# A two-layer graph network with mixing and experts: gates as sums on VectorE, row copies chunk by chunk, a table load moved, and zero products at three stage ends

## What is computed

```python
w = jnp.einsum('rb,bio->rio', att, basis)            # 30 bases, 2 relations
for r in range(NUM_RELATIONS):
    gate = jax.nn.sigmoid(x_j @ gate_w[r, :, 0])     # one number of each row and relation
    msgs.append(gate[:, None] * x_j @ w[r])
msg = jnp.where((edge_type == 0)[:, None], msgs[0], msgs[1])
agg = jax.ops.segment_sum(msg, row, num_segments=x.shape[0])
return agg + x @ root + bias
```

## Time and profile before

| | |
|---|---|
| Median of 3 runs | 1045.41 us (1041.83 to 1046.39) |
| Profiled execution, its own time | 1051.21 us |
| Span of the profiled execution | 1049.4 us |
| Mean granted clock of TensorE | 0.963 of 2.4 GHz |
| Busy: TensorE, VectorE, ScalarE, GpSimd | 93%, 51%, 38%, 9% of the span |
| Moved by transfers | 120.46 MB |

### The profile page before, as it was taken

The page is one execution under the profiler, slowest core; times in us unless marked ns, Lnnn a source line. Parts: engine busy times, 40 slices in busy tenths (PEclk is TensorE's granted clock), DMA queues, the critical chain, the costliest instruction groups (busy, mean ns, idle before and its releaser), DMA issues. The chain is left out here.

```text
span 1049.4 us, 12457 instructions
## 1 busy us (share of the span) xinstructions
PE 980.8 (93%) x4787; PEld 632.9 (60%) x4787; DVE 532.9 (51%) x1127; ACT 399.3 (38%) x671; POOL 90.1 (9%) x83
## 2 busy tenths in 40 slices
PE   3999999899999999989999899999999899999998
PEld 1545544276454475458777655789999554445665
DVE  5358887733145311234211464387877733558661
ACT  3368776231101110021111233348886554332340
POOL 0000000000020203011000000033342000013000
PEclk9698999999998999988999899999999899999999
DMA  9678998850000104032483200412200400220001
GB/s 314 232 305 312 356 385 319 325 206 1 1 1 0 51 1 161 1 115 106 161 303 138 79 8 1 142 32 74 81 1 1 161 0 4 83 81 1 1 1 49
DMA packets 50645, 120.46 MB, mean 115 GB/s; under 512 B 4616, under 2 KB 18698, under 8 KB 50570
## 3 DMA queue, kind: packets, MB, share of 16 engines
q1 hardware_dynamic: 50042, 118.34, 30.9%
q10 hardware_dynamic: 528, 1.05, 0.3%
HBM read 118.10 MB, written 1.28 MB: 114 GB/s over the span
## 5 line engine op out<-in xcount | busy, mean ns | idle before, releaser
L387 PE MATMUL PS<-AR 128*125 128x512 f32 (+9 forms) x1490 | 423.6, 441 | 11.1 <-issue 4.5
L387 PEld LDWEIGHTS PS<-AR 128*128 128x128 f32 (+3 forms) x1490 | 227.9, 194 | 181.9 <-issue 173.3
L417 PE MATMUL PS<-AR 128*32 128x512 f32 x576 | 89.9, 635 | 27.6 <-DMA AR<-in_basis 27.3
L1845 ACT ACTIVATE AR<-PS 128x500 f32<-128x500 f32 (+6 forms) x73 | 41.8, 577 | 165.3 <-PE PS L387 82.1
L1848 ACT ACTIVATE AR<-iota,AR 125x625 f16<-125x625 f16 x119 | 86.0, 809 | 33.7 <-PE PS L476 33.7
L1237 DVE TENSOR_SCALAR AR<-iota,AR 125x625 f16<-125x625 f16 x165 | 60.5, 443 | 22.0 <-PE PS L476 22.0
L417 PEld LDWEIGHTS PS<-AR 128*32 128x32 f32 x576 | 19.3, 111 | 78.1 <-issue 43.6
L474 PE MATMUL PS<-AR 125*125 125x512 f16 (+9 forms) x425 | 63.9, 309 | 1.3 <-issue 1.2
L474 PEld LDWEIGHTS PS<-AR 125*125 125x125 f16 x425 | 47.6, 146 | 21.3 <-issue 12.6
L2323 POOL TENSOR_TENSOR whl<-AR,whh 128x512 fp32r<-128x512 f32 x32 | 46.2, 1466 | 93.5 <-ACT whh L1845 93.5
L1706 DVE TENSOR_TENSOR HMl<-AR,HMh 128x626 fp32r<-128x626 f32 x64 | 49.8, 818 | 5.2 <-ACT HMh L1845 5.2
(11 more groups left out here) (288 smaller groups left out, 1423.0 us busy)
## 6 DMA issues: line engine op xcount, KB each, us to landing
AR<-in_basis SPq DMA_DIRECT2D x80, 768.0 KB, 7.9
AR<-in_L_ffn_W SPq DMA_DIRECT2D x20, 1024.0 KB, 7.5
AR<-in_L_gnn_Wh SPq DMA_DIRECT2D x8, 512.0 KB, 3.9
AR<-in_L_gnn_Wh SPq DMA_DIRECT2D x16, 256.0 KB, 4.3
AR<-in_L_mix_W_qkv SPq DMA_DIRECT2D x1, 3072.0 KB, 11.1
AR<-in_L_gnn_root SPq DMA_DIRECT2D x2, 1024.0 KB, 14.4
AR<-in_WkvT SPq DMA_DIRECT2D x1, 2048.0 KB, 12.0
AR<-in_L_gnn_W SPq DMA_DIRECT2D x1, 2048.0 KB, 8.5
```

The source lines that it names most:

```text
L387: ins = te.matmul(o, l, r, start=start and i == 0, stop=stop and i == len(pairs) - 1)
L417: ins = te.matmul(CB[32 * j:32 * j + 32, :], Am[:, l, m, 16 * (n % 2):16 * (n % 2) + 32], ring[:, at // 3, at % 3, :], start=m == quarter[ ...
L1845: return se.activation(o, i, ACT.Copy, scale=scale)
```

## The change

- **Gates of both layers** are no longer products. VectorE multiplies a chunk's rows with the gate's weights and sums them in the same instruction (`gate_rows`: two instructions of 512 columns for each chunk), and ScalarE takes the sigmoid, of all of layer 0 in one instruction, of layer 1 chunk by chunk. The weights come as 1024 numbers broadcast to 125 partitions, one transfer for each layer, the second behind GpSimd's adding of the first bias. The transfers of `bias1` and `bias2` move from the start to between pieces 40 and 41 of the basis.
- **Order in layer 1:** root2 waits for the copies of the turned chunks; VectorE copies a turned chunk ahead of the lower parts.
- **Rows split by chunks:** XH and XL move to `oG`, each chunk's upper part is copied right behind its norm, so GpSimd's lower parts follow chunk by chunk. The weights of expert 2, whose buffer lies there, are loaded behind the last sorting product.
- **Last chunk:** `turn2(4)` ahead of `logits(3)`.
- **Zero products** (`keep_on`, 512 columns of fp16 zeros): 5 ahead of `turn2(4)`, 8 ahead of the placing, 11 at the end of the experts, 10 behind the last head.
- **Sigmoid's table** is called for behind the norms ahead of the heads.
- In the first stage's end VectorE takes the sums of round 13 behind three of the last five additions of counts.

```diff
+        gl = sb("gl", [128, NT, 2])
+        gw = [ar(oB, 2, 512), ar(oB - 374, 2, 512)]
-        XH, XL = fr("XH", oZ, NT, 512, p=P), fr("XL", oZ + 2560, NT, 512, p=P)
+        XH, XL = fr("XH", oG, NT, 512, p=P), fr("XL", oG + 2560, NT, 512, p=P)
...
+            def keep_on(key, n, i):
+                u = psum.take(key, slot=i)
+                slot(u)
+                for _ in range(n):
+                    ins = te.matmul(sl(i, 0, 512, P), zer[0:P, 0:P], zer[0:P, :], start=True, stop=True)
+                ins.then_inc(u.sem, 1)
...
-            pe.wait_ge(d_gw, 16)
-            for c in range(NT):
-                if c < 4:
-                    combos(1, 3 * c, 3 * c + 3)
-                read(psum["xt", 0, c])
-                gates(0, c)
-            combos(1, 12)
+            combos(1)
...
             for c in (2, 3, 4):
                 layer1(c)
-                gate1(c - 2)
                 turn1(c - 1)
                 if c != 3:
                     mix_out(c // 2 + 1)
+            read(psum["xt", 1, 0])
             root2(0, bank[0])
-            gate1(3)
             turn1(4)
-            read(psum["l1", 1])
-            root2(1, bank[1])
-            gate1(4)
-            for c in (2, 3):
+            for c in (1, 2, 3):
+                read(psum["xt", 1, c])
                 read(psum["l1", c])
                 root2(c, bank[c])
+            read(psum["xt", 1, 4])
...
+            keep_on("on0", 5, next(i for i in range(2) if i not in (psum["l2", 4].slot, psum["xt", 2, 3].slot)))
+            turn2(NT - 1)
             logits(3)
-            turn2(NT - 1)
             logits(4)
             for f in psum.free:
                 for s, v in f:
                     pe.wait_ge(s, v)
+            keep_on("on1", 8, 0)
             pe.wait_ge(l0_read, NT)
...
                     back(r - 1, True)
+                    for _ in range(11):
+                        te.matmul(BH[0:P, :], zer[0:P, 0:P], zer[0:P, :], start=True, stop=True)
...
+            keep_on("on2", 10, 2)
             pe.wait_ge(wab_ready, 1)
...
+            def gate_rows(lay, c, scratch):
+                dv.wait_ge(gl_ready, lay * NT + c)
+                for r in range(2):
+                    ins = ve.tensor_tensor_reduce(out=scratch(r), in0=XN[0:P, c, :], in1=gw[lay][0:P, r, :], scale=1.0, scalar=0.0,
+                                                  op0=ALU.mult, op1=ALU.add, accum_out=gl[0:P, c, r:r + 1])
+                    if r == 0:
+                        dv.wait_ge(*step(ins))
+                ins.then_inc(gl_ready, 1)
...
                 if g + 2 < NS:
                     ends(g + 2)
+                if g < NT:
+                    dv.wait_ge(d_gw0, 16)
+                    dv.wait_ge(xn_ready, LN_X + g + 1)
+                    gate_rows(0, g, lambda r: sums[0][:, 0, 1:513])
...
-            combo_in(13)
             for b in range(NT):
                 added(FLUSHES - 1, b)
+                if b == 2:
+                    combo_in(13)
...
             mix_out(0)
+            gate1(0)
             mix_out(1)
+            gate1(1)
             for c in (2, 3, 4):
-                dv.wait_ge(gxh_ready, 2 * NT + 2 * (c - 2) + 2)
+                gate1(c)
+                if c in (2, 4):
+                    turned(("xt", 1, c - 1), c - 1, 4, XT)
                 for r in range(2):
                     gx_low(1, r, c - 2, 2 * NT + 2 * (c - 2) + r + 1)
-                if c in (2, 4):
-                    turned(("xt", 1, c - 1), c - 1, 4, XT)
...
-            for c in range(NT):
-                read(psum["gate", 0, c])
+            ac.wait_ge(gl_ready, NT)
+            act(gate[0:P, :, :], gl[0:P, :, :], ACT.Sigmoid).then_inc(gate_ready, 1)
+            ac.wait_ge(gate_ready, 1)
...
             def gate1(c):
-                gates(1, c)
-                read(psum["gate", 1, c])
+                ac.wait_ge(gl_ready, NT + c + 1)
+                act(gate[0:P, c, :], gl[0:P, c, :], ACT.Sigmoid).then_inc(gate_ready, 1)
+                ac.wait_ge(gate_ready, c + 2)
...
-            turned(("xt", 2, 4), 4, 4, XT)
-            full(("l2", 4))
-            for c in range(NT):
+                full(("z", 1, 1, 3))
                 ac.wait_ge(xn_ready, LN_L0 + c + 1)
                 copy(XH[:, c, :], XN[0:P, c, :]).then_inc(xh_ready, 1)
+            turned(("xt", 2, 4), 4, 4, XT)
...
                 ln_out(("a1", c), x1r, c, 128, LN_G1 + c + 1)
+            load_table(ACT.Sigmoid)
...
-            ye.dma_start(gw[:, :, :, :], A["gate_w"]).then_inc(d_gw, 16)
-            ye.dma_start(bias1, A["bias1"]).then_inc(d_bias, 16)
-            ye.dma_start(bias2, row(A["L0_gnn_bias2"]).to_broadcast([P, 512])).then_inc(d_bias2, 16)
+            load_gates(0, d_gw0)
             for n in range(5, 80):
                 load_basis(n)
+                if n == 40:
+                    sp.wait_ge(gl_ready, NT)
+                    ye.dma_start(bias1, A["bias1"]).then_inc(d_bias, 16)
+                    ye.dma_start(bias2, row(A["L0_gnn_bias2"]).to_broadcast([P, 512])).then_inc(d_bias2, 16)
...
+            sp.wait_ge(br_ready, 1)
+            sp.wait_ge(pool_x, NT)
+            load_gates(1, d_gw1)
             full(("l1", 4))
             ye.dma_start(WO, kp(A["L0_mix_W_out"])).then_inc(d_wo, 16)
+            sp.wait_ge(gl_ready, 2 * NT)
...
             load_expert(1)
-            load_expert(2)
...
+            full(("xs", 3))
+            load_expert(2)
```

More of the change, by code:

```diff
@@ L140, in build @@
         zer = sb("zer", [128, 512], F16)
-        gw = sb("gw", [128, 2, 4, 2])
+        gl = sb("gl", [128, NT, 2])
         gate = sb("gate", [128, NT, 2])
@@ L261, in build @@
         bank = [PS[0:P, 512 * c:512 * c + 512] for c in range(4)]
-        d_x, d_cst, d_iota, d_edge, d_att, d_gw = (sem("d_" + n) for n in ("x", "cst", "iota", "edge", "att", "gw"))
+        d_x, d_cst, d_iota, d_edge, d_att, d_gw0, d_gw1 = (sem("d_" + n) for n in ("x", "cst", "iota", "edge", "att", "gw0", "gw1"))
         d_bias, d_bias2, d_bout, d_route, d_head, d_r1e, d_r1, d_r2 = (
@@ L295, in build @@
             sem(n) for n in ("x_ffn", "wab_ready", "sc_ready", "num_exp", "num_ready", "x_mix"))
+        gl_ready, gate_ready = sem("gl_ready"), sem("gate_ready")
         pool_x, nm_ready, brh_ready, br_ready = (sem(n) for n in ("pool_x", "nm_ready", "brh_ready", "br_ready"))
@@ L402, in turn @@
                 ins.then_inc(u.sem, 1)
[L404 to L407, removed]
             def combos(n, a=0, b=len(PARTS)):
@@ L583, in turn1 @@
                 turn(("xt", 1, c), c, XN, 4, "dve" if c % 2 else "act")
-            def gate1(c):
-                read(psum["xt", 1, c])
-                gates(1, c)
             pe.wait_ge(d_wqkv, 16)
@@ L1389, in _, with gate1 @@
             mix_sum(0, 1)
+            def gate1(c):
+                dv.wait_ge(d_gw1, 16)
+                read(psum["l1", c])
+                gate_rows(1, c, lambda r: ar(oRING + 512 * (NT * r + c), 512, p=P))
             mix_out(0)
+            gate1(0)
             mix_out(1)
+            gate1(1)
             for c in (2, 3, 4):
-                dv.wait_ge(gxh_ready, 2 * NT + 2 * (c - 2) + 2)
+                gate1(c)
+                if c in (2, 4):
+                    turned(("xt", 1, c - 1), c - 1, 4, XT)
                 for r in range(2):
                     gx_low(1, r, c - 2, 2 * NT + 2 * (c - 2) + r + 1)
-                if c in (2, 4):
-                    turned(("xt", 1, c - 1), c - 1, 4, XT)
                 if c != 3:
@@ L1876, in _ @@
                 ln_root(c, LN_X + c + 1)
-            def gates(lay, c):
-                i = full(("gate", lay, c))
-                act(gate[0:P, c, :], sl(i, 0, 2, P), ACT.Sigmoid).then_inc(act_read, 1)
             def combo_out(k):
@@ L2358, in _, with load_gates @@
                 load_basis(n)
-            ye.dma_start(gw[:, :, :, :], A["gate_w"]).then_inc(d_gw, 16)
-            ye.dma_start(bias1, A["bias1"]).then_inc(d_bias, 16)
-            ye.dma_start(bias2, row(A["L0_gnn_bias2"]).to_broadcast([P, 512])).then_inc(d_bias2, 16)
+            def load_gates(lay, d):
+                ye.dma_start(gw[lay][0:P, :, :].rearrange("p r i -> p (r i)"), A["gate_w"][lay:lay + 1, :].to_broadcast([P, 1024])).then_inc(d, 16)
+            load_gates(0, d_gw0)
             for n in range(5, 80):
                 load_basis(n)
+                if n == 40:
+                    sp.wait_ge(gl_ready, NT)
+                    ye.dma_start(bias1, A["bias1"]).then_inc(d_bias, 16)
+                    ye.dma_start(bias2, row(A["L0_gnn_bias2"]).to_broadcast([P, 512])).then_inc(d_bias2, 16)
             sp.wait_ge(combo_done, 80)
@@ L2479 @@
     a["c_amask"] = (flat[:, :, None] // 30 == np.arange(16) + 16 * np.array([j for _, j in PARTS])[:, None]).astype(np.float32)
-    a["gate_w"] = np.stack([g["L0_gnn_gate_w1"], g["L0_gnn_gate_w2"]]).reshape(2, 2, 4, 128).transpose(3, 0, 2, 1)
+    a["gate_w"] = np.stack([g["L0_gnn_gate_w1"], g["L0_gnn_gate_w2"]]).reshape(2, 1024)
```

## The result

The changed kernel takes 1029.37 us (median of 4 executions, 1025.45 to 1032.42), the kernel before beside it 1045.22 (4 executions, 1041.83 to 1046.39): a ratio of 0.9851, 95% interval 0.9816 to 0.9886, 15.9 us faster. In a second, longer measurement it was 1028.56 against 1043.83, ratio 0.9836 (0.9801 to 0.9871). The forecast of 1022 was 7 us too low; range and sign were right. The two profiled executions differ by more, 22.1 us of span, because that of before stood 6 above its median. The sum of 23.9 therefore looked nearly right beside them; part by part it was not.

A forecast was written before the change was run, and what follows sets the result against it. TensorE's queue, busy 93% of the span, was taken as the bound. 5.0 + 8.6 + 7.0 + 1.0 + 2.3 + 0 = 23.9 us off 1051.2 gave 1027.3, 1021.5 against the median, so 1022; range 1010 to 1036.

The forecast's parts named there:

- sum of 23.9: Whole kernel: the gains in us of all six parts added, 5.0 + 8.6 + 7.0 + 1.0 + 2.3 + 0.
- A: First stage, layer 0's gates off TensorE: round 1 and the basis stream move earlier, net 5.0 us, ends 0 and 6.4.
- the 6.4: Round 1 of the first stage: without gates its last six products end at 37.3 instead of 43.75, 6.4 us earlier.
- the first stage gives nothing: Rival, chance 0.11: the stream catches up or VectorE's sums hold the one-hot tiles; the first stage gains 0, giving 1027.
- B: Layer 1's gates off TensorE: products 5.0, waits 1.0, clock 2.6; sum 8.6 us, ends 2.0 and 11.1.
- C: End of the second layer: struck routing steps, new order and clock held by zero products; 7.0 us taken, low end 1.2.
- No routing step over 0.3 us: Sign for the end of the second layer: no VectorE routing step longer than 0.3 us, against 1022 ns in the profile.
- D: End of the experts: 11 zero products fit the wait of 3.12; full clock gives 1.0 us, ends 0 and 1.9.
- E: Heads: sigmoid's table called earlier gives 1.3 us, the clock may give 1.0; sum 2.3, ends 0 and 2.9.
- F: Behind the last head: 10 zero products take 2.6 in a wait of 2.61; gain nothing, up to 2.6 lost at half clock.
- 1013 to 1031: Whole kernel: the forecast's own range in us, said to come from the ends for both layers' gates and the second layer's end.
- clock not held: Rival, chance 0.23: zeros or thin work may not keep the clock up; 10.4 us less gain, giving 1032.

The follow-up runs named there:

- after_c_undone: The changed kernel with the end of the second layer as before, without its 5 and 8 zero products: 1031.59 us, ratio 0.9874 to the kernel before.
- after_no_zeros: The changed kernel without any of its zero products (5, 8, 11 and 10): 1029.91 us, ratio 0.9841 to the kernel before.
- before_c: The kernel before with only the end of the second layer changed, zero products there included: 1048.36 us, ratio 1.0045 to the kernel before.
- before_a: The kernel before with only layer 0's gates as VectorE's sums, biases in mid-stream and combo_in(13) late: 1050.83 us, ratio 1.0056.

## Why the forecast was right, and where it was wrong

**A, gates of layer 0: wrong.** The step that failed is "the six products that need it then end at 37.3 at half clock: 6.4 us earlier", and under it the choice of 43.75 as the end of round 1 now. It was the end in an execution that had lost the clock; in the four that had not it is 38.3 to 40.8, no later than without the gates, so the 6.4 is nothing there. Against the usual first z product (207.0 to 209.7) the changed kernel's, 211.5 and 214.1, is 2 to 7 us **later**. That bound was missing from my range for A, whose low end was 0. What the 5.0 then missed is the stretch from round 7 to 10, some 5 us longer with A, for a cause that no run here settles. Round 2 at 43 brought z to 211 with A, and round 2 at 44 brought it to 207 without. The rival "the first stage gives nothing" was nearer than the forecast, and still too kind. That the clock might be a matter of the execution stood in one half sentence of mine ("its low-clock stretches may not all be in the median run") and was priced at half a microsecond; here it was 10. What VectorE's sums take was right: 20 of them with a mean of 691 ns.

**B, gates of layer 1: right, mis-sized.** 11.0 for 8.6, near the upper end of 11.1. From layer1(2) to the first z product it is 40.4 us, not 42 to 43. Two terms were too small. The waits are 1.10 and 0.72, not 1.3 and 1.7, so 2.2 us of the 4.0 went and not 1.0. With the gates' 5.0 that leaves 3.8 for the clock, where I took 2.6 of at most 5.1; it was 1.00 over all of the 40.4 us above. The weights of layer 1 held nobody.

**C, end of the second layer: right, mis-sized.** 5.2 us of 7.0 in the profiled pair, 4.1 by the median of after_c_undone. Up to the placing it gave 4.2 of the 4.9 forecast (68.8 us from the last z product, against 73.0), and 0.6 from there to the sorting. The sorting did not: the clock fell at 455.2, inside it, for 3.4 us, so it gave 0.4 us, not 2.5. The three struck steps of before took 1.02, 1.30 and 1.34 us (472.3 to 475.8), 3.0 us more than their usual 0.2 each, where I had 2.4. My theory that full-width zero products would keep the clock is therefore half right: without the zero products the half clock lasts 10 to 17 us in this place (six profiles), with them 3.4 to 6.8 (eight), but it isn't gone. "No routing step over 0.3 us" was wrong too. The fifth subtraction on GpSimd and a step of the routing on VectorE, each from its engine's timeline of after:

```profile
447.55 1.26 POOL L2322 TENSOR_TENSOR XL<-AR,XH 125x512 fp32r<-125x512 f32 x1 [15.24 <-ACT XH L1866]
```

```profile
447.58 1.26 DVE L1440 TENSOR_SCALAR sm<-cst,sc 125x8 f32<-125x8 f32 x1
```

Eight columns take 1.26 us, and end with the subtraction: VectorE's step was shut out until GpSimd's instruction ended. Of the three such strikes of before one is left, and a step of 0.65 beside a memset. The Trainium skill ("SBUF — State Buffer", Terms) calls the port pair that the two engines share a lock that is held for the whole instruction, with the loser blocked; the trace agrees, to 0.03 us.

**D and E, experts' end and heads: right.** 2.8 us of 3.3 in every profile that has both: 0.6 at the experts, and 2.1 in the heads, also without any zero product (119.2 to 117.1 us for the heads in after_no_zeros). The table now loads at 656.60, ahead of the turned rows:

```profile
656.60 1.28 ACT L1869 ACT_TABLE_LOAD   x1
657.90 0.20 ACT L1869 ACTIVATE zt<-eps 128x1 f32<-128x1 f32 x1
660.00 1.11 ACT L1869 ACTIVATE AR<-PS,gbe 128x500 f32<-128x500 f32 x2 [1.90 <-PE PS L861]
```

**F, behind the last head: right on the whole.** The rest takes 237.7 to 241.2 us with the ten products (eight profiles), 236.5 to 244.3 without (six). The 4.6 us that the profiled pair shows there are 1.7 of the shifted half clock and 2.9 of the thin products.

**The sum.** With the usual first stage in place of the earlier trace rows: A +4.6 (212.8 as the mean of the two profiles of the changed kernel, against 208.2 as that of the three untouched and undisturbed ones), B −11.0, C −5.2, D and E −2.8, the rest 0: −14.4, where −15.9 and −15.3 were measured. That the time fell in the range was partly luck: A was 9.6 too good, and B 2.4 too poor, and the two offset each other in part. The narrower range that I called "its own", 1013 to 1031, does not follow from the ends that I gave: with A, B and C all at them it is 1017 to 1039. Of the rivals, "clock not held" gave 1032, and is as near to 1029 as the forecast, but for a wrong reason: the clock was held in B, D and E.

## What to carry to other kernels

Before a sum is built on a half-clock stretch of a profile, ask whether the stretch belongs to the kernel or to that execution: the profiled one stood 6 us above its median, and a single stretch held more than that. Work taken out of the busiest engine's queue gives nothing where the engine then waits for data that come no earlier, and the rearranged work can cost something elsewhere: here some 5 us between two rounds much later, for a cause still open. Judge one part of a change by its own stretch between two fixed products (B's agrees within 0.1 us in ten profiles), not by the whole span, of which the last quarter alone, where nothing was changed but ten zero products, took 236.5 to 244.3 us.

## What the hardware showed that was not expected

- The clock can fall with TensorE busy nearly all of the time. In before_c it went to its lower level at 956.8 us, with TensorE busy for all of the 16.8 us ahead (matmuls waiting in the pipe counted); in the profiled execution of before it stayed at 1.00 over the same products.
- Executions of the kernel before went from 1037.8 to 1060.9 us on one chip (29 executions), far more than the 4.6 us between the first four timed. 17 of them lie between 1037.8 and 1045.4 at a granted clock of 0.970 to 0.977, 12 between 1049.3 and 1060.9 at 0.953 to 0.967, and none between; the execution profiled first (1051.2, 0.963) is of the second kind. The lost clock of the earlier trace rows may be one reason, but hardly the only one: before_a falls into two groups too, six and six, and none of the eight profiles with A shows that loss.
- TensorE stood still for 2.4 to 3.0 us with no releaser and the one-hot tiles there, beside a 16 KB packet of instructions in a full stream of data.
